# Projecting layer 0 in pairs of items with the weights standing in TensorE

## What is computed

```
# layer 0
xn = layernorm(x, g_in)
q = (xn @ Wq).reshape(b, n, H, DH).transpose(0, 2, 1, 3) * scale
kv = xn @ Wkv
k, v = (kv[..., :DH], kv[..., DH:])
k, v = concatenate([nk, k], axis=1), concatenate([nv, v], axis=1)
sim = einsum('bhid,bjd->bhij', q, k) + bias          # causal, then key mask
out = einsum('bhij,bjd->bhid', softmax(sim), v)
x = x + layernorm(out.transpose(0, 2, 1, 3).reshape(b, n, INNER) @ Wo, g_out)
# layer 1: the same, but q and k are divided by their norms (l2norm) and scaled,
# and the bias comes from a small network over relative positions
```

## Time and profile before

| | |
|---|---|
| median of 3 runs | 1322.88 us (1322.64 to 1322.96) |
| the profiled execution | 1320.26 us |
| its span | 1318.4 us |
| busy in the span | PE 97%, PEld 90%, DVE 84%, ACT 65%, POOL 60% |
| granted PE clock | 0.996 of full speed |
| DMA | 85.93 MB, mean 65 GB/s |

### The profile page before, as it was taken

The page is one execution under the profiler, slowest core; times in us unless marked ns, Lnnn a source line. Parts: engine busy times, 40 slices in busy tenths (PEclk is TensorE's granted clock), DMA queues, the critical chain, the costliest instruction groups (busy, mean ns, idle before and its releaser), DMA issues.

```text
span 1318.4 us, 28295 instructions
## 1 busy us (share of the span) xinstructions
PE 1281.4 (97%) x8152; PEld 1180.5 (90%) x8152; DVE 1103.8 (84%) x2948; ACT 861.5 (65%) x3246; POOL 796.4 (60%) x1382
## 2 busy tenths in 40 slices
PE   5799999999999999999999999999999999999997
PEld 5688889899999999999989999999999999999995
DVE  5788788878778778878789998998998998998986
ACT  4666656666667677676666676676676676676673
POOL 5553444434446666554567676676676676676673
PEclk9899999999999999999999999999999999999999
DMA  8301111024151221232623110110110110110101
GB/s 235 99 25 48 35 39 49 26 66 81 39 165 54 88 97 58 96 112 75 168 82 150 49 48 24 48 48 24 48 48 24 48 48 24 48 48 24 48 33 41
DMA packets 52216, 85.93 MB, mean 65 GB/s; under 512 B 7888, under 2 KB 22256, under 8 KB 51616
## 3 DMA queue, kind: packets, MB, share of 16 engines
q1 hardware_dynamic: 47168, 75.81, 18.8%
q0 software_dynamic: 4128, 9.03, 2.3%
q10 hardware_dynamic: 832, 0.04, 0.0%
HBM read 57.07 MB, written 27.79 MB: 64 GB/s over the span
## 4 chain that ended last, share of the span: by engine, by line
PE 89%; DVE 3%; issue 2%; DMA 2%; ACT 2%; POOL 1%; SPq 1%; POOLq 0%; DVEq 0%; ACTq 0%
PE bank_q L1359 30%; PE bank_y L1441 25%; PE bank_s L1296 12%; PE bank_o L1296 10%; PE bank_p L1408 6%; PE bank_t L1378 4%; PE bank_t L1340 3%; DMA wq_l<-wq_store 1%; ACT p_raw L814 1%; DMA x_in<-in_x 1%; DVE wq_raw L987 1%; PE bank_t L1386 0%; DVE pt_l L1183 0%; DVE qt_l L1116 0%; PE bank_t L1296 0%
## 5 line engine op out<-in xcount | busy, mean ns | idle before, releaser
L814 ACT ACTIVATE p_raw<-s_sb,neg_m 128x130 f32<-128x130 f32 (+1 forms) x1024 | 372.0, 366 | 137.5 <-DVE neg_m L1173 135.6
L653 POOL TENSOR_TENSOR p_sb<-p_raw,rden 128x256 f32<-128x256 f32 x256 | 157.5, 615 | 305.9 <-DVE rden L1179 305.9
L1359 PE MATMUL bank_q<-wq_h,xt_h 128*128 128x384 f32 x768 | 269.3, 351 | 7.0 <-DVE wq_l L950 3.4
L1359 PE MATMUL bank_q<-wq_h,xt_l 128*128 128x384 f32 x768 | 261.1, 340 | 0.0
L1359 PE MATMUL bank_q<-wq_l,xt_h 128*128 128x384 f32 x768 | 260.8, 340 | 0.0
L643 POOL TENSOR_TENSOR bias_g<-bias,mask_row 128x260 f32<-128x260 f32 x256 | 179.0, 699 | 108.8 <-DVE s_sb L1166 106.7
L1441 PE MATMUL bank_y<-wo_h,ot_h 128*128 128x512 f32 x512 | 218.2, 426 | 1.2 <-POOL wo_l L586 1.2
L1441 PE MATMUL bank_y<-wo_h,ot_l 128*128 128x512 f32 x512 | 201.7, 394 | 0.0
L1441 PE MATMUL bank_y<-wo_l,ot_h 128*128 128x512 f32 x512 | 201.4, 393 | 0.0
L814 ACT ACTIVATION_READ_ACCUMULATOR p_raw<-s_sb,neg_m 128x1 f32 x1024 | 192.3, 188 | 0.0
L1166 DVE TENSOR_TENSOR s_sb<-bank_s,bias_g 128x392 f32<-128x392 f32 x256 | 143.1, 559 | 34.5 <-PE bank_s L1296 30.4
(11 more groups left out here) (144 smaller groups left out, 3147.4 us busy)
## 6 DMA issues: line engine op xcount, KB each, us to landing
x_in<-in_x SPq DMA_DIRECT2D x32, 256.0 KB, 3.1
x_res<-in_x SPq DMA_DIRECT2D x32, 256.0 KB, 2.8
x_mid<-y_out SPq DMA_DIRECT2D x32, 256.0 KB, 2.1
x_in<-x_mid SPq DMA_DIRECT2D x32, 256.0 KB, 2.8
x_res<-x_mid SPq DMA_DIRECT2D x32, 256.0 KB, 2.7
out_x<-y_out SPq DMA_DIRECT2D x32, 256.0 KB, 2.1
wq_raw<-in_L_cond_Wq SPq DMA_DIRECT2D x4, 768.0 KB, 7.2
wq_store<-w_sb SPq DMA_DIRECT2D x6, 384.0 KB, 3.8
```

Of the source, the lines that this page charges most:

```text
L653: e.tensor_tensor(to[:, 0:2 * P].rearrange("p (e j) -> p e j", e=2), low_blocks(of)[:, :, 2:LOW], r[:, 0:2, :].broadcast_to([P, 2, P]), AL ...
L814: last = e.activation(p_raw[:, g % 2, lo:hi], s_sb[:, g % 2, lo:hi], ACT.Exp, bias=neg_m[:, h:h + 1], accum_out=esum[:, h:h + 1])
L1359: last = e.matmul(bank_q[p % 2][:, 0:hi - lo], a[:, c, :], b[:, c, lo:hi], start=(c == 0 and k == 0), stop=(c == KC - 1 and k == 2))
```

## The change

In layer 0 the projection is made for two items at once, with the weights standing in PE and both items' `xt` moving (256 columns). `project_group(m, g)` makes the queries of group g for items m and m+1 (24 matmuls), `project_kv` keys and values (12). Features come out on partitions, so ACT and DVE split queries and keys straight out of PSUM (`split_group`, `split_keys`); `transpose_q`, `transpose_k`, `q_nat`'s and `k_nat`'s copies are gone in layer 0. Values lie the wrong way now: ACT copies those of both items into `vt_sb`, one `transpose_v` turns them, and DVE writes `v_raw` (`values_back`). `xt`, `qt`, `kt` and `v_raw` have room for two items. Steps 0 to 29 become 15 pairs (`pair(at)`), each with a new order on each engine; all are unrolled. Pair s holds items 2s and 2s+1 and projects items 2s+2 and 2s+3. Steps 30 and 31 keep the order of `step` but project nothing of layer 0. Layer 1 keeps its steps. The opening normalises items 0 and 1 together (x of item 1 goes to `x_res`), and item 2 and 3's statistics are taken there. `wo_raw` shares its memory with `wq_raw` now, so the load of Wo waits for all of `wq_l`.

```diff
-FIRST, LAST = (13, 4), (15, B - 4)
+FIRST, LAST = 4, B - 4
+    for s in range(PAIRS - 1):
+        pair(item_of_pair(s))
+    straight(B - 2, B + FIRST)
+    with e.Fori(FIRST, LAST + 1) as i:
+        step(lambda d: (1, i + d))
+    straight(B + LAST + 1, N + 2)
...
-        wo_raw = sb("wo_raw", [P, OC, D])
+        wo_raw = wq_raw[:, :, :].rearrange("p c n -> p (c n)")[:, 0:OC * D].rearrange("p (c n) -> p c n", c=OC)
...
 # SP, opening
             load_x((0, 0))
+            e.dma_start(x_res[:, :], x[1]).then_inc(x1_loaded, 16)
             load_wq(0)
             load_mask(0)
             load_bias0(0)
             wait(e, xn_ready, (0, 0))
-            load_x((0, 1))
-            load_bias0(1)
-            wait(e, xn_ready, (0, 1))
             load_x((0, 2))
+            load_bias0(1)
+            for p in range(3):
+                e.wait_ge(wq_ready[p], KC)
             load_wo(0)
+            wait(e, xn_ready, (0, 2))
+            load_x((0, 3))
...
 # POOL
-                    e.wait_ge(q_psum[half], B)
+                    for last_reader in ((g_psum[0], g_psum[1]), (g_psum[1], g_psum[2]), (g_psum[3], kv_psum))[half]:
+                        wait_last_pair(e, last_reader)
...
 # ACT
+            def split_group(m, g):
+                wait_pair(e, g_psum[g], m)
+                wait(e, s_psum[g], m, -1)
+                e.activation(qt_h[:, :, g, :, :], bank_q[g % 2][:, :].rearrange("p (a u t) -> p a u t", a=2, u=2), ACT.Copy)\
+                    .then_inc(g_h_ready[g], 1)
...
 # PE
+            def project_group(m, g):
+                wait(e, xt_ready, m, 1)
+                wait_pair(e, g_ready[(g + 2) % G], m, -1 if g < 2 else 0)
...
+                out = bank_q[g % 2][:, :].rearrange("p (a u r i) -> p r a u i", a=2, u=2, r=2)
+                for r in range(2):
+                    features = slice((2 * g + r) * P, (2 * g + r + 1) * P)
+                    passes = []
+                    for c in range(KC):
+                        xh, xl = (t[:, c, :].rearrange("p (a u i) -> p a u i", a=2, u=2) for t in (xt_h, xt_l))
+                        wh, wl = (t[:, c, features] for t in (wq_h, wq_l))
+                        passes += [(wh, xh), (wh, xl), (wl, xh)]
+                    last = product(out[:, r, :, :, :], passes)
+                last.then_inc(g_psum[g], 1)
...
+            def transpose_v(m):
+                wait_pair(e, vt_copied, m)
+                wait_pair(e, pk_ready, m)
+                e.transpose(bank_t[:, 0:P], vt_sb[:, :], ident[:, :]).then_inc(vt_psum, 1)
...
+            def pair(at):
...
+                on(0, scores, 0)
...
+                on(0, scores, 1)
+                on(-1, attend, 1)
+                on(0, scores, 2)
+                on(-1, output, 0, 2)
+                on(3, transpose_x)
+                on(-1, output, 2, 4)
+                on(0, scores, 3)
+                on(1, scores, 0)
+                on(0, transpose_p, 0)
+                on(2, project_group, 1)
+                on(-1, output, 4, 6)
+                on(0, transpose_p, 1)
+                on(1, scores, 1)
+                on(-1, output, 6, 8)
+                on(0, net_slot)
+                on(2, project_group, 0)
+                on(0, transpose_p, 2)
+                on(1, scores, 3)
+                on(1, scores, 2)
+                on(2, project_kv)
+                on(0, attend, 0)
+                on(0, transpose_p, 3)
+                on(2, project_group, 3)
+                on(1, transpose_p, 0)
+                on(0, output, 0, 2)
+                on(0, attend, 1)
+                on(0, output, 2, 4)
+                on(1, transpose_p, 1)
+                on(2, transpose_v)
+                on(2, project_group, 2)
+                on(1, transpose_p, 2)
+                on(1, attend, 0)
+                on(4, transpose_x)
+                on(0, output, 4, 6)
+                on(1, transpose_p, 3)
+                on(0, output, 6, 8)
```

More of the change, by code:

```diff
@@ L108, in item_of, with item_of_pair, stream @@
     return lambda d: ((n + d) // B, (n + d) % B) if 0 <= n + d < N else None
-def stream(e, step, between=None):
+def item_of_pair(s):
+    return lambda d: (0, 2 * s + d) if 0 <= 2 * s + d < B else None
+def stream(e, pair, step):
     def straight(first, last):
         for n in range(first, last):
-            if between:
-                between(n)
             step(item_of(n))
[L120 to L124, removed]
+    for s in range(PAIRS - 1):
[4 more added lines that the diff above has]
+    straight(B + LAST + 1, N + 2)
 def build(nc, x, bias0, cond, mask0, mask1, g_in, null_bias, wq, wkv, wo, g_out, q_scale, k_scale,
@@ L474, in _ @@
                 e.dma_start(g_out_sb[:, layer, :], row(g_out[layer]).broadcast_to([P, D])).then_inc(g_out_loaded, 16)
[L475 to L486, removed]
+            stream(e, pair, step)
             e.wait_ge(x_stored, 16 * N)
@@ L721, in _ @@
             masked_bias((0, 0), 2)
-            stream(e, step, between)
+            stream(e, pair, step)
         @block.scalar
@@ L834, in on, with new @@
                         stage(at(d), *which)
-                on(1, split_xt)
+                def new(stage, *which):
+                    if at(1) is not None and at(1)[0] == 1:
+                        stage(at(1), *which)
+                new(split_xt)
+                on(0, exps, 0)
+                new(q_out, 0)
+                on(0, split_v)
+                on(0, exps, 1)
+                new(q_out, 1)
+                on(0, exps, 2)
+                on(0, split_pt, 0)
+                new(q_out, 2)
@@ L837, in step, with pair, on @@
+                on(-1, split_ot, 1)
+                new(split_qt, 0)
+                on(0, exps, 3)
+                on(0, split_pt, 1)
+                new(split_qt, 1)
+                on(0, split_pt, 2)
+                new(split_kt)
+                on(0, split_ot, 0)
+                on(0, split_pt, 3)
+            def pair(at):
+                def on(d, stage, *which):
+                    if at(d) is not None:
+                        stage(at(d), *which)
                 on(0, high_parts)
@@ L1157, in take_mask @@
                 wait(e, bias_ready[3], m, -1)
+                if m[0] == 0 and slot(m) == 0:
+                    wait(e, bias_ready[2], m, -1)
                 e.tensor_scalar(mask_row[:, 2:LOW], mask[:, m[0], m[1], :], -1.0, BIG, ALU.add, ALU.mult)\
@@ new lines, in project_kv @@
+            def project_kv(m):
+                wait(e, xt_ready, m, 1)
+                for b, done in ((8, TCOPY1), (10, PRE2), (14, TCOPY2), (16, TABLE)):
+                    if is_item(m, 0, b):
+                        e.wait_ge(net_step, done)
+                if is_item(m, 0, 0):
+                    e.wait_ge(wq_ready[2], KC)
+                passes = []
+                for c in range(KC):
+                    wh, wl = (t[:, c, INNER:QKV] for t in (wq_h, wq_l))
+                    passes += [(wh, xt_h[:, c, :]), (wh, xt_l[:, c, :]), (wl, xt_h[:, c, :])]
+                product(bank_t[:, 0:2 * P], passes).then_inc(kv_psum, 1)
@@ L1415, in attend @@
                     wait(e, v_ready, m)
+                if is_item(m, 0, 0) and half == 0:
+                    wait(e, xt_ready, m, 2)
                 wait(e, ot_ready[1 - half], m, -1 if half == 0 else 0)
@@ L1449, in on, with new @@
                         stage(at(d), *which)
-                on(1, transpose_x)
+                def new(stage, *which):
+                    if at(1) is not None and at(1)[0] == 1:
+                        stage(at(1), *which)
+                new(transpose_x)
                 on(0, scores, 0)
@@ L1477, in _ @@
             first = (0, 0)
             transpose_x(first)
-            for p in range(3):
-                project(first, p)
-            transpose_q(first, 0)
-            transpose_k(first)
-            transpose_q(first, 1)
-            stream(e, step)
+            transpose_x((0, 1))
+            project_group(first, 0)
+            transpose_x((0, 2))
+            project_group(first, 1)
+            project_kv(first)
+            stream(e, pair, step)
 _INS = ["x", "fside_16xSxS_0", "cond_64", "mask_BxS_bk0", "mask_BxS_bf1",
```

747 lines of the change are left out of this document (484 added, 263 removed).

## The result

The changed kernel takes 1318.01 us (median of 19 runs, 1314.66 to 1321.01), the kernel before 1320.45 on the same chips (19 runs, 1318.66 to 1324.73): ratio 0.9975, 95% interval 0.9967 to 0.9983. The forecast was 1297, with a range of 1283 to 1312: the time lies 6 us outside it. The profiled execution has a span of 1318.1 us, before 1318.4, so the two traces can be set against each other stage by stage.

The account below looks back on a forecast made before the run. PE's work was taken to bound layer 0 after the opening. Terms: -26.2 (items 2 to 29), +1.2 (opening), -0.9 (steps 30 and 31), layer 1 nothing; 1322.9 - 25.9 = 1297 us, range 1283 to 1312.

Parts of the forecast that it names:

- The products: Layer 0 projection matmuls: no gain, 12.6 us for two items before and after, with the same 27648 columns streamed.
- the turned queries and keys: Transpositions dropped from PE's path in layer 0: 0.99 us less an item, minus 0.11 for one `transpose_v` a pair.
- The pitch: Start-to-start distance of the new `bank_q` matmuls on PE, taken as 0.117 us from `bank_o`, which has the same form.
- rival 3: New `bank_q` matmuls are slower than 0.117 us; at 0.174 each the kernel stands at 1395 us; chance 0.04.
- Rival 1: `ot_l`, `pt_l` and `xt_l` on DVE come late, 1 to 1.5 us a pair: 1315, or 1308 us; chance 0.17.
- Rival 2: Loads of standing operands bound PE, 19.7 us an item: nothing gained in 28 items, 1323 us; chance 0.03.
- The 9.3 us of unsettled pairs: Excess of steps 2 to 29 over 28 settled steps of 19.71 us, claimed to stay.
- the sum for items 2 to 29: 14 pairs in layer 0: 28 x 0.99 - 14 x 0.11, 26.2 us less.
- Can the others follow at 18.8 us an item?: Check of DVE, ACT and POOL in a pair: DVE 83% busy, tightest places 0.5 to 1 us spare, costed at nothing.
- The opening: Start to pair 1: first scores 8.9 us later, near 36.5, pair 1 near 74.2, so 1.2 us more.
- the forecast's case: Forecast with its bounds, opening -4 to +6, steps 30 and 31 +-4: 1285 to 1306 us, chance 0.74.
- Steps 30 and 31: End of layer 0 and change to layer 1: 15 + 19.7 + 5.8 = 40.5 us against 41.41, 0.9 us less.

Follow-up runs that it names:

- e10: Version with all three repairs (store and raw weights moved, opening reordered, layer 1 weights fetched earlier; 1289.8 us), `transpose_v` done nine times instead of once: 1301.32 us.
- e4: On the changed kernel, DVE's opening splits weight parts 1 and 2 before it waits for x of item 2: 1311.22 us.
- e9: On the changed kernel, the bias table's 2 MB store is issued on ACT's queue at the start of pair 8, not by SP: 1311.26 us.
- e7: On the changed kernel, POOL fetches all three parts of layer 1's projection weights behind its last normalise of the last pair: 1312.83 us.

## Why the prediction was wrong

**Right.** The products cost nearly the same and the turned queries and keys were the gain: a settled pair takes 37.50 us with PE at 100%, 1.92 less than two steps before, 1.87 forecast. The pitch nearly held: 24 `bank_q` matmuls of a group take 2.85 to 3.0 us, 0.119 to 0.125 each where 0.117 was taken, so rival 3 is out. Rival 1 is out as a steady cost (PE idle for none of the settled pair). Rival 2 is out: PEld is busy 35.08 of 37.50 us in the pair, 93.5%, against 92.6% in a step before, and the time fell by 1.9 us. The rule in the Trainium skill (Perfetto Trace Analysis, Identifying the Most-Contended Engine), which judges PE's headroom by this share (and by the arithmetic done against the peak), would have had the change spend its last 7%; here the loads' printed times overlap, and e10 adds eight more and pays only their pitch. The 9.3 us of unsettled pairs stayed, 10.7 measured (550.85 - 15.2 - 14 x 37.5).

**The step that failed** is the sum for items 2 to 29, 26.2 us less. It rests on "Can the others follow at 18.8 us an item?", which went through the lists of DVE, ACT and POOL for a settled pair, left out SP's, and so put the waits for transfers in the pairs at nothing. Pair 8 isn't settled: there SP issues the table's store, moved from item 12 to item 16 (a move that the account of the change does not name either), and the raw weights behind it. The price was in the trace before: 23.3 us to landing, hidden in a gap of x loads that pairing made irregular. This is 15.2 of the 25.6 us that are missing between the two traces. (By medians less is missing, 23.5: the 19 runs before have a median of 1320.45, and the forecast was added to the 1322.88 of three of them.)

**Sizes that were off.** The opening: the first s_sb at 37.66, forecast 36.5; the first pair 41.4 from there, forecast 37.7, at a granted clock of 0.92 over the whole stretch; together 4.8 over, within the 6 that the forecast's case allowed; from trace to trace this moves by up to 3 us (see e4). Steps 30 and 31: step 31 26.2, forecast 25.5, and that is near by luck: PE waited 3.9 us for `wq_l` where 5.8 was forecast, and its own work took 21.7 us in place of 19.7, at a granted clock of 0.93. Step 30 18.35, forecast 15: PE waits 3.35 us there, 3.05 of them for one `p_sb`, and the 12.4 us of work that were worked out for it took 15.0, since the clock fell to 0.50 behind the wait. The text had put the clock into the opening's bounds alone. Together 3.4 + 0.7 over, 4.1. Layer 1 is 0.7 over, which no run explains.

**The range** held each of these but no loss as large as pair 8's: rival 1 at its worst was 1315. With only the table's store moved the kernel takes 1305.86 (one run, e2), inside it.

## What to carry to other kernels

When a change alters the rhythm in which transfers are issued, go through the issuing engine's list for every irregular iteration, with the time to landing of each large transfer beside the gap between the urgent ones; a store of 2 MB that was hidden in a regular rhythm may fit no longer. A settled iteration tells what a loop gains, not what its exceptions cost. And a pause of PE is to be priced with what the clock takes after it.

## What the runs showed that was not expected

- A 2 MB store from 16 partitions, in packets of 1 KB (1.99 MB in 1947 packets in e9's view), took 23 us at some 102 GB/s with the 16 DMA engines eight to nine tenths busy. Loads of the same size took 8.6 to 10.1 us in the changed kernel. It delayed x on another engine's queue too: that queue moved nothing for 8 us, and DVE waited 9.23 us (e9). What makes the store slow was not tried.
- SP, issuing into its queue while this goes on, is itself held: 17.79 us for three issues, 4.92 and 5.04 for single ones of 256 KB, where 0.43 is usual. In e9 it is held though the store is on ACT's queue.
- Three us without work (step 30) were followed by matmuls at a granted clock of 0.50; what had been worked out as 12.4 us of PE's work took 15.0.
- DVE's `v_l`, which reads two operands in SBUF, stood still for the length of POOL's unbroken row: 3.69 us in place of 0.36. The Trainium skill (SBUF — State Buffer, Summary: rules for kernel authors) says that of a DVE operation with two SBUF inputs and a GpSimd one that reads SBUF, the second to issue blocks until the first finishes; the trace agrees in that one of the two stood still, but `v_l`, which waited, is printed as the first to start (619.49, POOL's row 619.82), and the wait was for the end of the whole row of five, not of one instruction. With POOL's row broken up (e7) the same two took 0.36. One stretch shows this; a hole in POOL's list was worth some 3 us to DVE there.
